# Weighing a quarter of the exponentials of an attention in SBUF instead of out of the PSUM bank

## The reference

```python
Q, K, V = (proj(Wq, bq), proj(Wk, bk), proj(Wv, bv))        # 16 heads of 16
lam = LAMBDA_MAX * jnp.exp(-ALPHA * u_prev.reshape(Bb))
use_sparse = lam >= SPARSE_THRESHOLD
scores = jnp.einsum('bhqd,bhkd->bhqk', Q, K) * scale
bias = lam[:, None, None, None] * prior_bias[None, None]     # 0 or -1 by a mask of the prior
dense_out = einsum(softmax(scores + bias), V)
sparse_out = einsum(softmax(scores of K_SPARSE=32 listed keys per query), V of them)
out = where(use_sparse, sparse_out, dense_out) @ Wo.T + bo
```

## Time and profile before

| | |
|---|---|
| median of 3 runs | 1601.97 us (1601.73 to 1603.41) |
| the profiled execution | 1594.84 us, span 1593.0 us |
| TensorE (PE) busy | 1455.9 us, 91% |
| VectorE (DVE) busy | 1032.9 us, 65% |
| ScalarE (ACT) busy | 810.3 us, 51% |
| GpSimd (POOL) busy | 666.1 us, 42% |
| granted clock of TensorE, mean | 0.958 of 2.4 GHz |

### The profile page before, as it was taken

One profiled execution on the slowest core, in us unless ns is written; L12 is line 12 of the kernel. 1 busy time (PEld: TensorE's weight loads), 2 busy tenths in 40 slices (PEclk: granted clock), 3 DMA queues, 4 the chain that ended last, 5 costly groups with the idle time before them and its releaser, 6 DMA issues. The chain is left out here.

```text
span 1593.0 us, 21701 instructions
## 1 busy us (share of the span) xinstructions
PE 1455.9 (91%) x7649; PEld 693.1 (44%) x7697; DVE 1032.9 (65%) x2506; ACT 810.3 (51%) x975; POOL 666.1 (42%) x455
## 2 busy tenths in 40 slices
PE   4788999999999999888998878799999999999988
PEld 2513333332433332333343323345566567777745
DVE  8789878889767886665877493554451437667232
ACT  3753666787556666457765657733332134334101
POOL 5336799998769999613312012141000300000160
PEclk9759999999999999999999979799999999999999
DMA  2340010231311111113242022130000223544061
GB/s 80 122 132 9 27 41 29 89 80 56 80 34 47 38 39 27 35 35 83 91 115 74 21 71 71 55 101 3 1 0 24 93 70 111 177 153 135 28 121 28
DMA packets 74759, 104.52 MB, mean 66 GB/s; under 512 B 14843, under 2 KB 49092, under 8 KB 74650
## 3 DMA queue, kind: packets, MB, share of 16 engines
q1 hardware_dynamic: 70730, 96.66, 20.1%
q0 software_dynamic: 3072, 6.03, 1.9%
q10 hardware_dynamic: 848, 0.43, 0.1%
HBM read 72.39 MB, written 32.77 MB: 66 GB/s over the span
## 5 line engine op out<-in xcount | busy, mean ns | idle before, releaser
L1475 ACT ACTIVATE sb_prob<-wide,sb_ranges 128x1024 f32<-128x1024 f32 (+3 forms) x384 | 380.1, 1006 | 207.8 <-PE wide L2218 114.5
L1249 POOL TENSOR_TENSOR sb_prob<-sb_prob,sb_weight 128x1024 f32<-128x1024 f32 x192 | 448.9, 2363 | 73.1 <-ACT sb_prob L1475 70.9
L2213 PE MATMUL wide<-sb_stack_q,sb_stack_k 114*128 114x512 f16 (+3 forms) x896 | 282.4, 364 | 15.6 <-ACT sb_prob L1475 7.7
L1799 DVE CUSTOM_DVE_ANT_0 sb_junk<-bank,sb_bias 128x512 bf16<-128x512 f32 x345 | 230.4, 687 | 54.0 <-PE bank L2183 49.2
L1522 ACT ACTIVATE sb_sil<-wide,sb_weight 128x320 f32<-128x320 f32 (+1 forms) x128 | 77.5, 607 | 316.0 <-PE wide L2299 259.1
L2183 PE MATMUL bank<-sb_stack_k,sb_stack_q 112*128 112x512 f16 (+3 forms) x601 | 217.2, 378 | 20.5 <-DVE sb_rowmax L1799 5.7
L2233 PE MATMUL wide<-sb_prob,sb_v_aug 128*17 128x512 f32 (+3 forms) x1792 | 223.6, 564 | 10.3 <-ACT sb_o_raw L1487 8.8
L2299 PE MATMUL wide<-sb_weight,sb_ffn 128*128 128x512 f16 x768 | 181.4, 388 | 9.2 <-DVE sb_act_s L2012 7.3
L2012 DVE SCALAR_TENSOR_TENSOR sb_act_s<-wide,sb_weight,sb_sil 128x512 f32<-128x512 f32 x64 | 47.9, 749 | 186.8 <-ACT sb_sil L1522 172.8
L1254 POOL TENSOR_SCALAR_AFFINE_SELECT sb_prob<-sb_prob 128x256 f32<-128x256 f32 x128 | 53.0, 420 | 244.6 <-ACT sb_prob L1475 244.5
L2183 PEld LDWEIGHTS bank<-sb_stack_k,sb_stack_q 112*128 112x128 f16 x601 | 58.8, 98 | 205.4 <-issue 91.3
(11 more groups left out here) (311 smaller groups left out, 1921.2 us busy)
## 6 DMA issues: line engine op xcount, KB each, us to landing
o_raw<-sb_o_raw SPq DMA_DIRECT2D x32, 256.0 KB, 2.2
sb_weight<-rg SPq DMA_DIRECT2D x8, 1024.0 KB, 4.8
sb_xT<-ru SPq DMA_DIRECT2D x8, 1024.0 KB, 4.8
sb_big<-rd SPq DMA_DIRECT2D x8, 1024.0 KB, 6.2
parts<-sb_o_norm SPq DMA_DIRECT2D x40, 128.0 KB
sb_stack_q<-parts SPq DMA_DIRECT2D x32, 128.0 KB, 3.2
sb_stack_k<-parts SPq DMA_DIRECT2D x32, 128.0 KB, 3.2
sb_o_norm<-o_raw SPq DMA_DIRECT2D x64, 64.0 KB, 2.2
```

The lines of the kernel that those rows point to most:

```text
L1249: e.tensor_tensor(p, p, weight_of(*u[1:]), ALU.mult).then_inc(weigh_p.handle, 1)
L1475: e.activation(p[:, :, first:HALF], sc[:, :, first:HALF], ACT.Exp, scale=unscale).then_inc(SC.empty_sem(u), 1)
L1799: e.tensor_tensor_reduce(out=junk[:, i % 2, 0:hi - lo], in0=BK.tile(u)[:, 0:hi - lo], in1=bias[:, qt, lo:hi], scale=1.0, scalar=-3e38, op0 ...
L2213: i = e.matmul(sc[:, j * HALF + first:(j + 1) * HALF], stack_k[0:ROWS_M, n % 3, pair, kt * P:(kt + 1) * P], stack_q[0:ROWS_M, n % 3, PAIRS ...
```

## The change

ScalarE treats VectorE's units like GpSimd's: it writes the exponential into the probability buffer in SBUF and frees the wide tile itself. VectorE then weighs in place in the buffer, with the same instruction (minimum, then multiplication), and reports on a signal of its own, `weigh_d`. The products with the values, and those loads and mixer steps that overwrite the weights, wait on `weigh_d` in place of the wide tile's mark or `exp_a`, which is gone. Which engine weighs which unit, the order of work and the buffers stay.

```diff
-        exp_a = signal("act_exp_wide", [u for u in of("score") if JOBS[u[1]][0] == 0 and not to_pool(*u[1:])])
+        weigh_d = signal("dve_weigh", [u[1:] for u in of("weigh")])
...
         def unit_ready(n, u):
             if on_diagonal(n, *place(n, u)[0:2]):
                 return capped_p.after((n, u))
-            return weigh_p.after((n, u)) if to_pool(n, u) else SC.emptied(("score", n, u))
+            if JOBS[n][0]:
+                return SC.emptied(("score", n, u))
+            return weigh_p.after((n, u)) if to_pool(n, u) else weigh_d.after((n, u))
...
                 elif kind == "mixload":
-                    w.wait_ge(SC.emptied(list(exp_a.value)[-1]))
+                    w.wait_ge(weigh_d.end)
                     w.wait_ge(weigh_p.end)
...
                 elif kind == "mod":
                     if not b:
                         w.wait_ge(weigh_p.end)
-                        w.wait_ge(SC.emptied(list(exp_a.value)[-1]))
+                        w.wait_ge(weigh_d.end)
...
                     unscale = exp_scale[:, JOBS[n][0] * B + JOBS[n][1]]
-                    if u in exp_a.value:
-                        e.activation(sc, sc, ACT.Exp, scale=unscale).then_inc(exp_a.handle, 1)
-                        continue
                     for mark in prob_vacant(u[1:]):
                         w.wait_ge(mark)
                     e.activation(p[:, :, first:HALF], sc[:, :, first:HALF], ACT.Exp, scale=unscale).then_inc(SC.empty_sem(u), 1)
...
-                    w.wait_ge(exp_a.after(key_))
+                    w.wait_ge(SC.emptied(key_))
                     w.wait_ge(weight_ready(n, v))
-                    for mark in prob_vacant((n, v)):
-                        w.wait_ge(mark)
-                    e.scalar_tensor_tensor(out=p, in0=heads_of(SC.tile(key_)[:]), scalar=HUGE, in1=weight_of(n, v),
-                                           op0=ALU.min, op1=ALU.mult).then_inc(SC.empty_sem(key_), 1)
+                    e.scalar_tensor_tensor(out=p, in0=p, scalar=HUGE, in1=weight_of(n, v), op0=ALU.min,
+                                           op1=ALU.mult).then_inc(weigh_d.handle, 1)
```

## The result

Before the kernel took 1601.85 us (median of 4 runs, 1598.9 to 1603.41), after 1618.04 us (4 runs, 1615.14 to 1622.06): 1.0105 times as long, with a 95% interval of 1.0079 to 1.0131. The change makes the kernel 16 us slower; 49 us were forecast. The profiled execution of after took 1618.66 us (span 1616.9), that of before 1594.8 us (span 1593.0), 24 us less.

What follows compares the result with a forecast made beforehand. The prediction took TensorE as busiest in the prior attention (518.8 of 547 us), with GpSimd setting the pace in tight places. Weighing 45, bank -4 and passing over 8 gave +49 on 1602, so 1651 us, range 1610 to 1705.

Steps and rivals of the forecast that it cites:

- Exponential, semaphores: ScalarE writing SBUF (1.6 us on an idle engine) and products and loads waiting on VectorE's new signal: both cost nothing.
- Bank: Score banks come free behind ScalarE, 1.22 us earlier: gain at most 12 us, a third taken, 4 us.
- weighing less relief: In the prior attention, cost of turn-taking minus the gain from earlier free banks: 45 - 4 us.
- Weighing: VectorE's 64 weighings with two SBUF inputs take turns with GpSimd: 25 to 64 us, middle 45 us taken.
- The lower end: Per stretch of the prior attention, only the larger excess over GpSimd's or VectorE's idle time counts: 25 us.
- The estimate by that rule: By the skill's lock rule, a weighing waits only for the instruction in progress: 65 us for VectorE, +41 us in all.
- Being passed over: A VectorE weighing is not let in between GpSimd's weighings and TensorE stands: one event taken, 8 us.
- Put on the median: The +49 us put on before's median of 1602 us, with everything after the prior attention only shifting.
- What would show it: Signs: weighings 2.4 us on the mean, GpSimd's towards 2.7, stage some 50 us longer, score wait gone, clock dips.
- Absorbed in part: Rival: idle time of GpSimd and VectorE takes up part of the cost, +13 us, 1615 us; chance 0.14.
- Passed over often: Rival: every eighth VectorE weighing loses 8 us, +105, 1707 us, or 1675 with half as many; chance 0.2.
- the two without a loss: Rivals: earlier free banks make it faster, 1590 to 1598 us (0.07); gain and loss cancel, 1602 us (0.04).

Runs made afterwards that it cites:

- one_input: Changed kernel, but VectorE takes a maximum over the probability buffer (one SBUF input) instead of weighing, exponentials taken of 0: 1594.19 us, 0.9974 of before.
- late_bank: Changed kernel, but the wide PSUM tile of VectorE's units is freed only behind the weighing, as before the change: 1635.63 us, 1.025 of before.
- the pair of added reads: Before, with one more VectorE instruction ahead of each of its 64 weighings, reading SBUF twice (1707.54 us) or once (1647.7 us).
- The second profiles: Before and the changed kernel, each unchanged and profiled once more: 1603.55 us and 1607.1 us, stage ends 660.7 and 687.5.
- fin_one_after: Changed kernel with line 1876's small instruction made a maximum over one input in the stage's eight jobs: 1605.44 us, ratio 1.0123.
- fin_one_before: Before with line 1876's small instruction made a maximum over one input in the stage's eight jobs: 1570.42 us, ratio 0.99; again on another chip 1574.99 us.
- more_vector: Before with four units each of jobs 5 and 7 given from GpSimd to VectorE: 1593.93 us, ratio 0.995.
- extra_one: Before with one more VectorE instruction ahead of each of its 64 weighings, a maximum reading one SBUF input: 1647.7 us, ratio 1.0326.

## Why the prediction was wrong in its size

*Exponential, semaphores: right.* `one_input` keeps both and is not slower.

*Bank: right for the old weighing.* A third of the 12 us, 4 us; `one_input` gave 3.8. But the prices are not independent: with the slow weighing the same relief is worth 12 us (`late_bank`). Only weighing less relief is well determined, and the two are compared together below.

*Weighing: the mechanism right, the size by 7 us too large.* Two inputs from SBUF make the two engines take turns: by the rows of after, by `one_input` and by the pair of added reads. For VectorE I counted 1.26 us each and it was 0.89. For GpSimd I counted 1.0 us for each of 64, and it was 0.88 us for 48, 42 us in all. Weighing less relief was put at 45 - 4 = 41 us, from the middle of 25 and 64; with the holds of line 1876 taken out of both kernels it measures 34.4 us. The lower end, reckoned by stretches, was 2.0, 3.3, 5.1, 3.6, 0, 1.3, 6.5 and 3.1 us, and the jobs grew by 2.0, 3.4, 5.8, 1.2, 0.3, 3.3, 7.7 and 2.9 (the stretches of the earlier trace rows and the jobs do not start at the same times, so single pairs agree only roughly). The stretches told where the loss would lie. That their sum, 25 us, is so near to the 26.6 is luck: less the relief it is 21 us, and what it has to be held against is 34.4. The last job shows what they had wrong: the 4.9 us that GpSimd had free there were the stall behind the long hold itself, and could take up nothing. Without the holds that job takes 55.7 us before and 63.5 after, 7.8 more and not 3.1.

The Trainium skill ("SBUF — State Buffer", section "Who interferes with whom") says that the shared pair is an exclusive lock: who issues first has it for the whole instruction, and the other blocks fully. The weighings agree: holds of 1.5 us ahead of 1.2 us of work, none over 3.06 us in all. The hold of 7.18 us in before goes beyond it. The estimate by that rule in the prediction, +41 us with nobody passed over, was nearer than mine, since it left out the step that failed.

*Being passed over: this step failed.* It said that a weighing that goes in would add one more event of 8 us. There was none: the longest weighing took 3.06 us. And the one event that before has is gone: at its place the small instruction took 0.72 us in place of 7.18. The runs without the holds price it: the stage grows by 34.4 us when neither kernel has them, by 26.6 as the kernels are, so that the change takes away 7.8 us of stall of which I had expected it to add 8. The second profiles give 32.7 and 687.5 - 660.7 = 26.8, so 5.9 us; the surest part is the 4.9 us of the last job. The step was wrong by 15.8 us (14 by the second profiles), the largest term. I had written the reason down, that a weighing breaks up GpSimd's unbroken runs, and drew it only as far as the cost for the weighing, not for what stood in those runs already.

The stage's sum: 49 forecast = 26.6 measured + 15.8 for this step + 6.6 for the weighing.

*Put on the median: 10 us more.* The stage grew by 26.6 us and the profiled executions by 24, but the medians lie 16 us apart, and 21 on the other chip. I had put the sum on the median as if later stages took the same time in each execution. They don't: the profiled execution of before is 7 us below its median, and the second one, at 1603.55, lost its time after the stage at a granted clock of 0.83 to 0.94. Such a fall isn't before's alone, as the second profile of after shows. But over all runs on that chip before's median clock is 0.959 and after's 0.9625, so before seems to lose somewhat more of this kind; the two ranges overlap. By time multiplied by clock the change costs 28 us, close to the stage, and without the holds 34 us (1549.6 less 1515.2, `fin_one_after` and `fin_one_before`), as the stage does. What makes the clock fall there in one execution and not in another stays open.

*What would show it.* The weighing's mean was to be 2.4 us (2.11), the longest over 3 (3.06), GpSimd's 2.7 (2.58), the stage +50 (+26.6), the score matmuls' wait gone (gone), those for row maxima and for GpSimd grown (grown). The granted clock was to dip where TensorE stands; over the stage it is 0.99 in both, and in the last job it rose from 0.94 to 1.00.

*The rivals.* "Absorbed in part", at 1615 us, came nearest in number (1618), for half of its reason: its 25 us less relief would be 13, the stage gave 26.6, and the clock took the rest back. "Passed over often" fell, as did the two without a loss.

**Open.** Why the small instruction of the last job is not let in at the ends of GpSimd's weighings in five profiles, while 64 weighings of after were let in at the first end at the latest, is not settled. In the first profile of before GpSimd's ends lie 0.19, 2.51, 4.81 and 7.10 us behind its start, and it gets in at the last, where GpSimd has run out of work; in other jobs the same instruction got in between two weighings of an unbroken run. Order and timing around it matter, as `more_vector` and `extra_one` show, but no run varied the timing alone. Also open are the clock after the stage and the split of the 51 us of `extra_one`.

## What to carry to other kernels

Before turning one of VectorE's inputs from PSUM to SBUF, look whether GpSimd reads SBUF at the same time: a small instruction that reads SBUF twice there already, and its longest duration against its shortest, is the probe. Then see by stretch, against what GpSimd and VectorE have free in each, where it will cost; but idle time that is itself the wake of a stall takes up nothing. And ask which stall of the kernel before the new order takes away as well as which it adds. When a stage's gain or loss doesn't arrive in the median, compare the granted clock of the same piece of later work before looking for a new wait.

## What the runs showed of the hardware that was not expected

A VectorE instruction with both inputs in SBUF can be passed over by GpSimd: 0.20 us of work took 7.18 and 7.19 us in the two profiles of before and 7.18 to 7.50 in three variants, over two ends of a weighing and a third just behind its start, at the same instruction; none of the 64 weighings of after was (longest 3.06 us, 1.22 alone). A weighing that goes in between two of GpSimd's costs GpSimd 0.86 us although it takes 1.22 by itself, so a part of it seems to lie in the hand-over; that is argued, not shown. And in different executions of one kernel the same piece of work ran at a granted clock of 1.00 and of 0.94, 101 and 107 us.
